# Layer 0's attention: a group's first pass issued beside the second pass of the group ahead, scores by single heads, taps by halves with diagonals made on GpSimd

## The reference

```python
qkvo = jnp.einsum('oc,bchw->bohw', qkvo_w[:, :, 0, 0], x) + qkvo_b[:, None, None]
lepe = lax.conv_general_dilated(v_ch, lepe_w, window_strides=(1, 1), padding='SAME', feature_group_count=C, dimension_numbers=('NCHW', 'OIHW', 'NCHW')) + lepe_b[:, None, None]
attn = jax.nn.softmax(SCALE * jnp.einsum('bnqd,bnkd->bnqk', q, k), axis=-1)
res = jnp.einsum('bnqk,bnkd->bnqd', attn, v)
res = res + lepe
out = jnp.einsum('oc,bchw->bohw', proj_w[:, :, 0, 0], res * o) + proj_b[:, None, None]
```

## Time and profile before

| | |
|---|---|
| median of 3 runs | 11625.7 us (11618.77 to 11634.1) |
| the profiled execution's own time | 11628.75 us |
| its span | 11626.7 us |
| busy: PE, PEld | 9232.0 us (79%), 4375.3 us (38%) |
| busy: DVE, ACT, POOL | 7331.4 us (63%), 5279.4 us (45%), 4048.5 us (35%) |
| mean granted TensorE clock | 0.799 of 2.4 GHz |
| image 0's layer 0, no scan beside it | until 820 us |

### The profile page before, as it was taken

The page is one execution under the profiler, slowest core; times in us unless marked ns, Lnnn a source line. Parts: engine busy times, 40 slices in busy tenths (PEclk is TensorE's granted clock), DMA queues, the critical chain, the costliest instruction groups (busy, mean ns, idle before and its releaser), DMA issues.

```text
span 11626.7 us, 100618 instructions
## 1 busy us (share of the span) xinstructions
PE 9232.0 (79%) x34200; PEld 4375.3 (38%) x34200; DVE 7331.4 (63%) x5589; ACT 5279.4 (45%) x7930; POOL 4048.5 (35%) x1678
## 2 busy tenths in 40 slices
PE   6867888788887888788887888868888788887656
PEld 2223333443334333443334433344333443334433
DVE  3228566855667655765658665586566855667892
ACT  3434554445543455434554355533554445543441
POOL 0015323523344333442335332353233523344560
PEclk8777778777788777888778987778778887788778
DMA  0012112321123211331114211141112321123231
GB/s 33 8 50 79 43 48 79 114 67 48 48 98 93 70 45 45 110 94 50 48 48 127 87 48 52 59 124 64 48 48 78 110 73 45 51 93 95 87 106 45
DMA packets 423033, 802.02 MB, mean 69 GB/s; under 512 B 226128, under 2 KB 241872, under 8 KB 422352
## 3 DMA queue, kind: packets, MB, share of 16 engines
q1 hardware_dynamic: 422480, 795.13, 21.3%
HBM read 698.28 MB, written 71.04 MB: 66 GB/s over the span
## 4 chain that ended last, share of the span: by engine, by line
PE 55%; DVE 20%; ACT 9%; issue 9%; DMA 3%; ACTq 1%; SPq 1%; DVEq 1%; POOL 1%; POOLq 0%
PE ps L910 9%; PE ps L891 7%; PE ps L762 7%; DVE R L1667 7%; PE ps L989 6%; PE ps L871 5%; DVE ps L1659 5%; PE ps L986 5%; ACT ps L1169 3%; DVE nmx L1595 3%; PE ps L1074 3%; PE ps L900 3%; PE ps L1057 2%; PE ps L972 2%; PE ps L962 2%
## 5 line engine op out<-in xcount | busy, mean ns | idle before, releaser
L1380 POOL TENSOR_TENSOR R<-R 128x1024 f32<-128x1024 f32 x1536 | 3644.5, 2373 | 5846.9 <-DVE ps L1659 5820.4
L1667 DVE TENSOR_TENSOR_SCAN R<-R,ps 128x1024 f32<-128x1024 f32 x1536 | 3512.1, 2286 | 1202.5 <-ACT R L1254 1065.7
L1254 ACT ACTIVATE R<-R,negA 128x1024 f32<-128x1024 f32 x1536 | 1752.0, 1143 | 1573.6 <-DVE R L1667 1466.3
L989 PEld LDWEIGHTS ps<-ident,R 128*128 128x128 f32 x12288 | 1662.3, 162 | 1129.0 <-issue 777.9
L989 PE MATMUL ps<-ident,R 128*128 128x128 f32 x12288 | 1886.9, 309 | 222.5 <-POOL R L1380 180.6
L1659 DVE TENSOR_TENSOR ps<-R 128x1024 f32<-128x1024 f32 x1536 | 1969.2, 1282 | 63.3 <-DVE R L1667 7.4
L871 PE MATMUL ps<-R 32*128 32x512 f32 x3072 | 1280.1, 1017 | 541.1 <-ACT ps L1169 505.7
L1595 DVE TENSOR_REDUCE nmx<-ps 128x2 f32<-128x1024 f32 x768 | 923.6, 1217 | 1061.0 <-PE ps L871 1053.0
L1194 ACT ACTIVATE R<-ps 128x1024 f32<-128x1024 f32 x768 | 784.9, 1022 | 1534.6 <-PE ps L891 1534.6
L1169 ACT ACTIVATE ps<-ps,nmx 128x512 f32<-128x512 f32 x1536 | 1009.0, 657 | 974.6 <-DVE nmx L1595 971.0
L986 PE MATMUL ps<-R,ident 128*128 128x512 f32 x1440 | 983.8, 820 | 342.9 <-ACT R L1244 336.4
(11 more groups left out here) (161 smaller groups left out, 5973.1 us busy)
## 6 DMA issues: line engine op xcount, KB each, us to landing
R<-bc_scratch SPq DMA_DIRECT2D x1024, 512.0 KB, 3.8
R<-in_x SPq DMA_DIRECT2D x72, 512.0 KB, 7.0
out<-R SPq DMA_DIRECT2D x72, 512.0 KB, 4.0
R<-shift_scratch SPq DMA_DIRECT2D x48, 640.0 KB, 10.4
R<-R SPq DMA_DIRECT2D x192, 128.0 KB
R<-out SPq DMA_DIRECT2D x48, 512.0 KB, 8.4
R<-in_w_qkvo SPq DMA_DIRECT2D x32, 576.0 KB, 9.5
rows_scratch<-R SPq DMA_DIRECT2D x24, 512.0 KB, 3.9
```

What stands on the lines that cost most here:

```text
L989: mm = pe.matmul(ps[:, 4 + b // 4, (b % 4) * P:(b % 4 + 1) * P], state[i % HELD][:, b * P:(b + 1) * P], ident[:, :], start=fresh and i % G ...
L1254: act.activation(decay[i % len(decay)], dt[:, c, :], ACT.Exp, scale=negA[:, col:col + 1]).then_inc(a_sb.h, 1)
L1380: pool.tensor_tensor(state[i % HELD], state[i % HELD], rows_c[slot], ALU.mult).then_inc(hc_sb.h, 1)
L1667: v.tensor_tensor_scan(h, a, b, 0.0, ALU.mult, ALU.add).then_inc(h_sb.h, 1)
```

## The change

Scores are made by single heads in both passes (one matmul per event: 64 `S` and 64 `T` per group), and the table of times is laid out anew. Group 0's first pass stands alone (12 steps). Then the second pass of group g (28 steps) stands beside the first pass of group g+1 (25 steps); the last group's second pass stands alone again (22 steps). Banks: `S` in 0 and 1 by turns, `T` in bank 2 alone beside a first pass and in 2, 0, 1 by turns in the last group, `V` and the taps in bank 3. Bank 3 holds one half of the queries at a time, so `V` goes by halves and every tap is done twice, once per half, each time with a diagonal of its own, now made on GpSimd in place of ScalarE (`diagonal`, 150 per image, four buffers). `O` takes out a half. `tv` goes to banks 0 and 1 after the maxima's row. `q2` moves the queries of the next group early; the keys' moves (`k2`) for groups 1 and 2 wait for the last `T` of the group ahead. Attention ends two steps earlier in the table (step 163 after 165).

```diff
-SB = 4 * LB
-TB = 2 * LB * (GH // 2)
+SB = 2 * LB * GH
+TB = 2 * LB * GH
+TAPS = 25
...
-S_STEPS, N_STEPS, T_STEPS = 9, 3, 20
-DIAGS = 8
+S_FIRST, S_STEPS, T_STEPS, T_LAST = 12.0, 25.0, 28.0, 22.0
+DIAGS = 4
...
+def first_pass(g, at, steps, late_max, late_sum):
+
+    ev = []
+    for n in range(SB):
+        t = at + n * steps / SB
+        ev += [(t, ("S", SB * g + n)), (t + late_max, ("R", SB * g + n)), (t + late_sum, ("P", SB * g + n))]
+    ev += [(at + 3.0, ("q2", g))] + ([(at + 3.5, ("k2", 0))] if g == 0 else [])
+    at += steps + 0.4
+    return ev + [(at, ("N1", g)), (at + 0.02, ("N2", g)), (at + 0.7, ("N3", g)), (at + 0.72, ("N4", g)), (at + 1.4, ("N5", g)),
+                 (at + 1.45, ("N", g)), (at + 2.0, ("M", g)), (at + 2.1, ("mr", g)), (at + 2.15, ("tv", g)),
+                 (at + (2.2 if g == 0 else 3.0), ("pv", g))]
...
+def second_bank(a):
+
+    return 2 if a < (GROUPS0 - 1) * TB else (2, 0, 1)[a % TB % 3]
...
+    ev += first_pass(0, at, S_FIRST, 0.15, 0.32)
+    at += S_FIRST + 2.8
...
-        for n in range(SB):
-            t = at + n * S_STEPS / SB
-            ev += [(t, ("S", SB * g + n)), (t + 0.30, ("R", SB * g + n)), (t + 0.32, ("P", SB * g + n))]
-        ev += [(at + (3.0 if g == 0 else 0.3), ("q2", g))]
-        at += S_STEPS + 0.1
-        ev += [(at, ("N1", g)), (at + 0.02, ("N2", g)), (at + 0.7, ("N3", g)), (at + 0.72, ("N4", g)), (at + 1.5, ("N5", g)),
-               (at + 1.55, ("N", g)), (at + 2.0, ("M", g)), (at + 2.1, ("mr", g))]
...
-        at += N_STEPS - 0.1
-        apart = T_STEPS / TB
+        last = g == GROUPS0 - 1
+        steps = T_LAST if last else T_STEPS
+        if not last:
+            ev += first_pass(g + 1, at + 0.4, S_STEPS, 0.35, 0.60)
+        apart = steps / TB
         for j in range(TB):
             t = at + apart * j
-            ev += [(t, ("T", TB * g + j)), (t + 0.02, ("E", TB * g + j))]
-            if j % 2:
-                ev += [(t + apart + 0.01, ("V", (TB * g + j) // 2))]
-        ev += [(at + 0.5 + 0.7 * j, ("dg", g, j)) for j in range(25)]
-        ev += [(at + 4 * apart + 0.7 * j + 0.3, ("dw", g, j)) for j in range(25)]
-        ev += [(at + T_STEPS + apart + 0.2, ("O", g))]
-        at += T_STEPS + 1
+            ev += [(t, ("T", TB * g + j)), (t + (1.0 if last else 0.5) * apart + 0.005, ("E", TB * g + j))]
+            if j % GH == GH - 1:
+                ev += [(t + 2.2 * apart, ("V", (TB * g + j) // GH))]
+        half = steps / 2
+        for hf in range(2):
+            for j in range(TAPS):
+                t = at + half * hf + 6.4 * apart + (half - 5 * apart) * j / TAPS
+                ev += [(t - 1.6, ("dg", g, TAPS * hf + j)), (t, ("dw", g, TAPS * hf + j))]
+            ev += [(at + half * (hf + 1) + 1.8 * apart, ("O", 2 * g + hf))]
+        at += steps + 0.2
+        ev += [(at, ("k2", g + 1))] if not last else []
+        at += 1.2
...
-            reader = ("E" if ev[0] == "T" else "P", ev[1])
+        if ev == ("p2",) or (ev[0] in IN_BANK0 and ev[1] in IN_BANK0[ev[0]]):
+            reader = (readers[ev[0]], *ev[1:])
         if ev == reader:
...
-        pT = [side(at, K1).rearrange("p (j q) -> p j q", j=2) for at in (3072, 4096, 5120, 12288)]
-        q2 = [[side(at, K1) for at in pair] for pair in ((10240, 11264), (6144, 11264), (6144, 7168))]
+        pT = [side(at + HALF * j, HALF) for at in (3072, 4096, 5120, 12288) for j in range(2)]
+        q2 = [[side(at, K1) for at in pair] for pair in ((10240, 11264), (0, 6144), (1024, 7168))]
...
-        diag = [[side(6144 + K1 * g + P * i, P) for i in range(DIAGS)] for g in range(GROUPS0)]
+        diag = [[side(9216 + K1 * g + HALF + P * i, P) for i in range(DIAGS)] for g in range(GROUPS0)]
...
-                        sp.wait_ge(pv_ps.h, pv_ps.at(img, 2 * LB * g))
+                        sp.wait_ge(t_ps.h, t_ps.at(img, TB * (g - 1) + 1))
...
+                if kind == "k2":
+                    g = c
+                    if g:
+                        sp.wait_ge(t_ps.h, t_ps.at(img, TB * g))
+                    for r in range(GH):
+                        rows = slice(64 * (r % 2), 64 * (r % 2) + HD)
                         sp.dma_start(k2[r // 2][rows, :], k4[HD * r:HD * r + HD, g, :]).then_inc(q2_in.h, 16)
...
-                    g, qc, hf, pair = a // SB, a % SB // 4, a % 4 // 2, a % 2
+                    g, qc, hf, r = a // SB, a % SB // 8, a % 8 // 4, a % 4
...
-                    if a >= 2:
+                    if a % SB >= 2:
                         pe.wait_ge(s_sum.h, s_sum.at(img, a - 1))
-                    if a % SB == 0 and g:
-                        pe.wait_ge(t_exp.h, t_exp.at(img, TB * g))
-                    if a % SB == 1 and g:
-                        pe.wait_ge(o_sb.h, o_sb.at(img, g))
-                    for r in (2 * pair, 2 * pair + 1):
-                        mm = pe.matmul(ps[:, r, :], q4[HD * r:HD * r + HD, g, qc * P:(qc + 1) * P],
-                                       k4[HD * r:HD * r + HD, g, hf * HALF:(hf + 1) * HALF], start=True, stop=True)
-                    mm.then_inc(s_ps.h, 1)
+                    elif g:
+                        pe.wait_ge(lv_sb.h, lv_sb.at(img, g))
+                    pe.matmul(ps[:, a % 2, :], q4[HD * r:HD * r + HD, g, qc * P:(qc + 1) * P],
+                              k4[HD * r:HD * r + HD, g, hf * HALF:(hf + 1) * HALF], start=True, stop=True).then_inc(s_ps.h, 1)
...
-                    g, kb, qh, pair = a // TB, a % TB // 4, a % 4 // 2, a % 2
-                    bank = 0 if scans else 4 * (a % 2)
-                    if a % TB == 0:
+                    g, qh, kb, r, n = a // TB, a % TB // 32, a % 32 // 4, a % 4, a % TB
+                    if n == 0:
                         pe.wait_ge(n_row.h, n_row.at(img, g + 1))
                         pe.wait_ge(q2_in.h, q2_in.at(img, 16 * (4 + 8 * (g + 1))))
                         pe.wait_ge(mr_in.h, mr_in.at(img, 64 * (g + 1)))
-                    if scans and a:
+                    if second_bank(a) == 2 and g < GROUPS0 - 1:
+                        if a:
+                            pe.wait_ge(t_exp.h, t_exp.at(img, a))
+                    elif n == 0:
                         pe.wait_ge(t_exp.h, t_exp.at(img, a))
-                    if not scans and a >= 2:
-                        pe.wait_ge(t_exp.h, t_exp.at(img, a - 1))
-                    for j in range(2):
-                        rows = slice(64 * j, 64 * j + HD + 1)
-                        mm = pe.matmul(ps[:, bank + j, :], k2[pair][rows, kb * P:(kb + 1) * P],
-                                       q2[g][pair][rows, qh * HALF:(qh + 1) * HALF], start=True, stop=True)
-                    mm.then_inc(t_ps.h, 1)
+                    elif n < 3:
+                        pe.wait_ge(lv_sb.h, lv_sb.at(img, NC))
+                    else:
+                        pe.wait_ge(t_exp.h, t_exp.at(img, a - 2))
+                    rows = slice(64 * (r % 2), 64 * (r % 2) + HD + 1)
+                    pe.matmul(ps[:, second_bank(a), :], k2[r // 2][rows, kb * P:(kb + 1) * P],
+                              q2[g][r // 2][rows, qh * HALF:(qh + 1) * HALF], start=True, stop=True).then_inc(t_ps.h, 1)
...
-                    g, kb, qh = a // (2 * LB), a % (2 * LB) // 2, a % 2
-                    if kb == 0 and qh == 0:
-                        pe.wait_ge(lv_sb.h, lv_sb.at(img, g + 1))
-                    pe.wait_ge(t_exp.h, t_exp.at(img, 2 * a + 2))
+                    g, qh, kb = a // (2 * LB), a // LB % 2, a % LB
+                    if kb == 0 and a:
+                        pe.wait_ge(o_sb.h, o_sb.at(img, a // LB))
+                    pe.wait_ge(t_exp.h, t_exp.at(img, GH * a + GH))
                     for r in range(GH):
-                        mm = pe.matmul(ps[HD * r:HD * r + HD, 2 + qh, :], vT[:, kb, P * g + HD * r:P * g + HD * r + HD],
-                                       pT[(2 * a + r // 2) % 4][:, r % 2, :], start=kb == 0, stop=kb == LB - 1,
-                                       skip_group_check=True)
+                        mm = pe.matmul(ps[HD * r:HD * r + HD, 3, :], vT[:, kb, P * g + HD * r:P * g + HD * r + HD],
+                                       pT[(GH * a + r) % 8], start=kb == 0, stop=kb == LB - 1, skip_group_check=True)
                     mm.then_inc(pv_ps.h, 1)
...
-                    m = a
+                    m, hf, tap = a, j // TAPS, j % TAPS
                     vp = vpad.rearrange("p (h w) -> p h w", w=36)
-                    pe.wait_ge(dg_sb.h, dg_sb.at(img, 25 * m + j + 1))
-                    for hf in range(2):
-                        win = vp[:, j // 5 + 16 * hf:j // 5 + 16 * hf + 16, j % 5:j % 5 + WW]
-                        mm = pe.matmul(ps[:, 2 + hf, :], diag[m][j % DIAGS], win, start=False, stop=False,
-                                       skip_group_check=True)
-                    mm.then_inc(dg_ps.h, 1)
+                    if j == 0:
+                        pe.wait_ge(lv_sb.h, lv_sb.at(img, m + 1))
```

(44 more changed lines are left out.)

63 lines of the change are left out of this document (32 added, 31 removed).

## The result

| | before | changed |
|---|---|---|
| median | 11629.9 us (4 runs, 11618.77 to 11634.14) | **13540.55 us** (4 runs, 13486.86 to 13558.82) |
| ratio, 95% interval | | 1.1637 [1.1602, 1.1672] |
| span of the profiled execution | 11626.7 us | 13548.5 us |
| mean granted clock | 0.799 | 0.775 |
| image 0's layer 0, until | 820.0 us | 1260.8 us |

The sign is as forecast, the size is not: +655 us were forecast and +1911 measured, and 13541 lies outside the range of 11900 to 12700. In the fourth period one image adds 1017.5 - 800.6 = 217 us, less 4.5 us by which the scan steps from 165 to the end became shorter (132.6 against 137.1). Taken seven times, with image 0's 441 us, that is 1928; the two profiled executions are 1922 apart. The changed kernel's seven periods are not alike, as those before are: this stretch takes between 990 and 1041 us, 1019 in the mean.

What follows compares the result with a forecast made beforehand. TensorE's work was taken to bound second passes, the score-maximum-exponential round first passes. From 11628.75 us, +546 for seven images beside a scan and +113 for image 0 gave 12288, forecast as 12285 us; range 11900 to 12700.

Steps and rivals of the forecast that it cites:

- What bounds the kernel, and the price of a matmul: Attention: TensorE's work bounds second passes, the round bounds first passes; a single 512-column matmul costs 1.05 us at 2.4 GHz.
- The step that failed: Merged stretches: every single S and T priced at 1.05 us, at the fast clock, giving 287 and 260 us.
- the terms laid on top of the matmuls' sum of 247: Merged stretches: 7 us for the start, 27 once for the column sums, 6 for the steps between groups.
- Image 0: Layer 0 with no scan beside it: merged stretches of 213 us each, 692 us against 579, +113 us.
- The lone first pass: Group 0's first pass, alone beside the scan: 141 us including the steps for the row sums.
- The round: Lone first pass: score (1.13 or 2.07 us by the clock), maximum, exponential and handovers in turn, 3.0 to 3.9 us.
- The last second pass: Last group's second pass, 22 steps alone: 169.5 us of work plus 7 and 6, 182.5 us.
- The two steps after it: Two scan steps that now run after the shortened attention stretch, at 4 us each.
- ScalarE, VectorE, GpSimd and SP at no cost: Added work and waits on these engines priced 0; upper bounds 30 us a period for GpSimd, 11 for SP.
- The rivals: Four other outcomes: array sharing (0.15), faster through more sharing (0.06), crossing waits (0.15), no change (0.03).
- rival 1: S and T in different halves of the array's rows overlap: 47 us less a period, 11914 us; chance 0.15.
- The waits: Merged stretches: T, exponentials and maxima wait on one another, TensorE losing 1.5 us a step, some 12875 us; chance 0.15.

## Why the prediction was wrong in size

By its own steps:

- **What bounds the kernel, and the price of a matmul**: right, at the fast level. The timeline after has singles at 1.05 us to the next start, V at 1.00, sums at 1.82, states at 0.93 to 1.02 (0.97 forecast), half taps at 0.96 to 1.08 (1.0).
- **The step that failed** is the one that priced every single at that level: "TensorE busy above 95% at a granted clock near 1 there", in the merged stretches. Busy above 95% held; the clock was 0.72 and 0.83. The stretches took 360 and 300.5 us, not 287 and 260, 113 us a period. (At 2.4 GHz they would be 259 and 249, so the terms laid on top of the matmuls' sum of 247 were 28 and 11 us too high, which hid part of the error.) I had read in the earlier trace rows that the busy stretches have the fast clock and the idle ones the slow one, and took idleness for the cause. But in those rows a stretch with idle time is also one of 32-row scores, and a busy one has taps, V and states of 128 rows beside its T. The rows before could not tell the two apart; the runs do, in both directions (128 rows at 26 to 30% idle: 0.88 to 0.98; scores of 32 and 33 rows between half taps, without a gap: 0.52 and 0.54 in image 0).
- **Image 0** is the same step: 371.9 and 377.4 us at 0.52 and 0.54, where 213 each were forecast. That makes 323 of the 328 us by which +113 fell short.
- **The lone first pass**: 162.6 us at 0.61, forecast 141. With S on 128 rows it is 138.1 at 0.93, so this term too was right but for the clock. The round had allowed a score both levels; at 2 us a score TensorE is busy 87% of the stretch and sets its pace.
- **The last second pass**: 186.8 against 182.5. **The two steps after it**: 7.5 us, less the 4.5 by which the rest became shorter, so 3 in place of 8.
- Summed up: (73 + 40 + 22 + 4 - 5) x 7 = 938, and 328, make 12288 into 13554; the profiled execution took 13550.4.
- **ScalarE, VectorE, GpSimd and SP at no cost**: right. TensorE idles 11 and 2 us in the two merged stretches. A maximum takes 0.686 us (0.68 forecast), E 0.60 (0.66), a diagonal 0.51 (0.30 to 0.97). A product of the scan (L1400) stands late behind diagonals and makes VectorE wait 167 us in all; TensorE waits for none of it in the merged stretches, and with the diagonals on ScalarE, where this wait is gone, the time was longer.
- **The rivals**: none of them came. S and T never start together in the changed kernel, where they are of 32 and 33 rows; that they do at 64 and 33 says that rival 1 failed by the shapes, not by the order. The waits did not cross. The profile of "what would show it" had the right entry, the clock near 1, and no rival stood behind it: with the clock of the first passes, 0.6, the merged stretches would be 478 and 433 us, 364 a period more and some 14800 in all. As a rival, that would have carried the range over what was measured.

What stays open: in every merged kernel of these runs group 0's merged stretch has a lower clock than group 1's with the same shapes (0.79 against 0.96 with pairs and zeros). How the clock goes with the rows between 32 and 128 is not known: 64 rows lifted it in some stretches and not in others. And the split of the 0.19 us between a drain and the load of weights was not tried.

The Trainium skill (TensorE: Matmul & The Clock Gate, Part 1) says that the clock is set by how busy the engine has been. This case does not agree as far as busy means without a gap: the earlier trace rows fit that reading, and the changed kernel's merged stretches, busy 97 to 99% at 0.72 and 0.83, do not.

## What to carry to other kernels

Read the granted clock of a stretch together with the rows that its matmuls use, and price a new stretch at the clock of a stretch with the same rows at work, not of one equally busy. Matmuls of a quarter of the rows should stay in pairs that stand side by side; where banks make that impossible, padding the contraction with zero rows is worth a try: it bought back clock in one stretch here (15.6 us) and cost nothing in the others. Filling TensorE's idle time with work of another stage is worth having (577 us here at nearly equal clock), but not at the price of the pairs (1314 us).

## What the runs showed of the hardware

- TensorE held without a gap, on 32- and 33-row matmuls between half taps, has 1.2 GHz for most of the time (0.52 in image 0); the same order with S on 128 rows has 0.96 and 0.99 beside a scan. With nothing but scores, in image 0: 0.53 on pairs of 32 rows at 90% busy, 1.00 on 128 rows at 78%.
- Rows of zeros can count as rows at work: 0.88 to 0.96 and 15.6 us of a 247.6 us stretch, though 0.78 to 0.79 in the stretch ahead of it.
- A 512-column float32 matmul takes 0.86 us to the next start among neighbours of the same rows, 0.95 with another shape on one side, 1.05 with one on both; at 1.2 GHz 2.00 with both. 33 and 64 rows count as one shape (0.85), 33 and 32 as two.
- Matmuls of two different streams ran side by side (starts 0.01 us apart) as 33 and 64 rows in different halves of the array, and never as 33 and 32 (of 3072 records of S 561 and none start within 0.2 us of a T's).
